# Reordering the first and last images of a fused GroupNorm, routed convolution and sign convolution kernel on one Trainium2 core

## What is computed

```python
# x = x + silu(bn(sum_e routing[b, e] * conv3x3(gn(x), w_experts[e])))
pooled = jnp.mean(x, axis=(2, 3))                       # x is gn(x) here
routing = jax.nn.sigmoid(pooled @ w_route.T + b_route)  # 4 experts
y = conv(x, w_experts)                                  # 3x3, 128 -> 4 * 128 channels
out = jnp.einsum('beohw,be->bohw', y, routing)
out = out * inv + (bn_beta - bn_mean * inv)
return jax.nn.silu(out)
# x = x + conv3x3(gn(x), sign(W))                       # 3x3, 128 -> 128 channels
```

## Time and profile before

| | us |
|---|---|
| median of 3 runs | 283.71 |
| lowest, highest of the 3 | 283.13, 285.51 |
| profiled execution, its own time | 283.86 |
| span of the profiled execution | 282.1 |
| TensorE busy (MATMUL records) | 270.5 (96%) |
| VectorE busy | 248.1 (88%) |
| ScalarE busy | 209.4 (74%) |
| GpSimd busy | 40.9 (15%) |

### The profile page before, as it was taken

One profiled execution on the slowest core, in us unless ns is written; L12 is line 12 of the kernel. 1 busy time (PEld: TensorE's weight loads), 2 busy tenths in 40 slices (PEclk: granted clock), 3 DMA queues, 4 the chain that ended last, 5 costly groups with the idle time before them and its releaser, 6 DMA issues.

```text
span 282.1 us, 3920 instructions
## 1 busy us (share of the span) xinstructions
PE 270.5 (96%) x1298; PEld 184.6 (65%) x1298; DVE 248.1 (88%) x443; ACT 209.4 (74%) x413; POOL 40.9 (15%) x58
## 2 busy tenths in 40 slices
PE   5599989999999999999999999999999999999896
PEld 5445755858576675858586776858586766757454
DVE  5697979899999999999999999999999999992832
ACT  2756888987879798988869898888878785618240
POOL 2100011212112021212123021212111031202000
PEclk9999999999999999999999999999999999999999
DMA  6999813461634544353625545353626455401312
GB/s 223 395 390 294 330 55 74 107 118 74 112 114 76 149 76 108 83 109 86 121 94 74 151 76 149 51 104 87 129 81 99 125 77 149 72 3 19 59 74 74
DMA packets 11252, 34.14 MB, mean 121 GB/s; under 512 B 1248, under 2 KB 3552, under 8 KB 11232
## 3 DMA queue, kind: packets, MB, share of 16 engines
q0 software_dynamic: 3888, 14.16, 29.6%
q1 hardware_dynamic: 7056, 19.47, 18.4%
q10 hardware_dynamic: 288, 0.26, 0.3%
HBM read 11.34 MB, written 15.73 MB: 96 GB/s over the span
## 4 chain that ended last, share of the span: by engine, by line
PE 78%; ACT 7%; issue 5%; DVE 5%; DMA 3%; POOL 1%; POOLq 0%; ACTq 0%; DVEq 0%
PE pc L457 35%; PE pa L422 12%; PE pe_ L422 11%; PE pb L422 11%; PE pd L412 6%; DMA X<-y 2%; DVE U L837 1%; ACT junk_mid L567 1%; DMA X<-x 1%; PE ps L395 1%; ACT hi L678 1%; DVE parts L803 1%; PE ps L390 1%; PE pb L457 1%; ACT dev L582 1%
## 5 line engine op out<-in xcount | busy, mean ns | idle before, releaser
L457 PE MATMUL pc<-lo,ws 128*128 128x496 f16 (+5 forms) x288 | 64.7, 371 | 0.0
L457 PE MATMUL pc<-hi,ws 128*128 128x496 f16 (+5 forms) x288 | 62.7, 372 | 1.0 <-ACT hi L678 1.0
L837 DVE SCALAR_TENSOR_TENSOR U<-we,route,U 128x1152 f32<-128x1152 f32 x45 | 63.4, 1410 | 0.1
L457 PEld LDWEIGHTS pc<-hi,ws 128*128 128x128 f16 x288 | 28.0, 98 | 32.3 <-issue 1.1
L457 PEld LDWEIGHTS pc<-lo,ws 128*128 128x128 f16 x288 | 28.3, 106 | 25.5 <-DVE lo L948 0.3
L422 PE MATMUL pa<-V,UM 128*128 128x256 f32 (+1 forms) x180 | 41.7, 382 | 0.0
L422 PE MATMUL pe_<-V,U 128*128 128x256 f32 (+1 forms) x180 | 40.6, 375 | 0.0
L422 PE MATMUL pb<-V,UM 128*128 128x256 f32 (+1 forms) x180 | 40.5, 375 | 0.0
L422 PEld LDWEIGHTS pb<-V,UM 128*128 128x128 f32 x180 | 34.2, 190 | 5.3 <-issue 0.4
L337 POOL TENSOR_TENSOR rstd<-ve,nhalf 128x2 f32<-128x2 f32 (+1 forms) x19 | 15.2, 803 | 154.0 <-ACT ve L595 154.0
L422 PEld LDWEIGHTS pe_<-V,U 128*128 128x128 f32 x180 | 34.1, 190 | 3.8
(11 more groups left out here) (97 smaller groups left out, 374.6 us busy)
## 6 DMA issues: line engine op xcount, KB each, us to landing
X<-x SPq DMA_DIRECT2D x15, 512.0 KB, 5.2
out<-X SPq DMA_DIRECT2D x14, 512.0 KB, 2.6
out<-ev POOLq DMA_DIRECT2D x14, 512.0 KB, 5.4
X<-y POOLq DMA_DIRECT2D x13, 512.0 KB, 4.6
we<-w_experts SPq DMA_DIRECT2D x3, 768.0 KB, 8.0
out<-X SPq DMA_DIRECT2D x3, 256.0 KB, 2.0
ws_raw<-w_sign SPq DMA_DIRECT2D x1, 576.0 KB, 11.5
X<-x ACTq DMA_DIRECT2D x2, 128.0 KB, 2.9
```

What stands on the lines that cost most here:

```text
L457: mm = mm_(rows[:, r0 - first // W:r1 - first // W, c0:c1], ws[:, tap * C:(tap + 1) * C], (hi, lo)[part][i % 2][:, r0 + ky - 1:r1 + ky - 1 ...
L837: v.scalar_tensor_tensor(out=flat(U[i % RING][:]), in0=flat(we[:, e, :, :]), scalar=route[:, i, e:e + 1], in1=flat(U[i % RING][:]), op0=AL ...
```

## The change

It touches the first 45 us of the program and its last image; the loop for t = 2 to 14 keeps its order on TensorE, ScalarE and GpSimd.

1. Dummy products: 9 at the start, 2 between `group_means(0)` and `group_vars(0)`, 4 behind `group_vars(0)`, 8 behind `route_logits(0)`. None stands behind `group_vars(1)` any more.
2. `group_means(1)` moves ahead of `route_logits(0)`. `group_vars(1)` moves behind the first two direct products (both halves of part 0).
3. VectorE forms `first_dev` and, from it and `rstd`, `pooled` of image 0 itself, instead of ScalarE's `zr` and `pool_routes(0)`. It also writes rows 17 to 31 of the first `xn` (`first_low_rows`), which ScalarE did. The five batch norm instructions are spread between the mixes of part 2. `pool_routes(2)` goes ahead of `mix(1, 3)`.
4. Image 0's second statistics on ScalarE: `squares`, `deviation` and the `IN` spread of chain 3 and `sign_weights` go ahead of `var_mid(0)`; `copy_minus(1)` comes last of them. `var_in(3)` moves from behind `mean_mid(0)` to ahead of `bias(2, IN)`. VectorE does `mix(2, 1)` before the inversion of image 1, no longer behind it, and `residual(0)` between `all_rows(2)` and `inner_rows(2)`. The first `hi` is written in two halves.
5. Image 14's residual moves from VectorE to the accumulating DMA (`DVE_RESIDUAL = (0, B - 1)`).
6. Last chain: ScalarE takes the sums from its Silu (`accum_out`), forms the mean (`last_mean`) and takes the variance in two halves (`last_variance`); VectorE's `part_stats` and `aggregate` of image 15 go away. On TensorE `group_means(18)` moves four products forward and `group_vars(18)` four.

```diff
-WARM = (7, 3)
+WARM = (9, 2, 4, 8)
...
-        DVE_RESIDUAL = (0, B - 2, B - 1)
+        DVE_RESIDUAL = (0, B - 1)
...
             group_means(0)
+            warm(WARM[1])
             group_vars(0)
+            warm(WARM[2])
+            group_means(1)
             route_logits(0)
-            group_means(1)
-            group_vars(1)
-            warm(WARM[1])
+            warm(WARM[3])
             direct_part(0, 0, 0)
             direct_part(0, 0, 1)
+            group_vars(1)
             direct_part(0, 1, 0)
...
+                elif t == B - 1:
+                    sign_half(t - 1, 0, 0)
+                    sign_half(t - 1, 0, 1, TAP_ORDER[:5])
+                    group_means(c + 1)
+                    sign_half(t - 1, 0, 1, TAP_ORDER[5:])
+                    sign_half(t - 1, 1, 0, TAP_ORDER[:5])
+                    group_vars(c + 1)
+                    sign_half(t - 1, 1, 0, TAP_ORDER[5:])
+                    sign_half(t - 1, 1, 1)
...
+            def last_mean():
+                i, c = B - 1, CHAINS - 1
+                act.wait_ge(silu_ready, silus(i) - 1)
+                activation(last_nm[:], ysum[:, i:i + 1], ACT.Identity, bias=nm[:, i, IN:IN + 1],
+                           scale=-1.0 / (HW * ROOT_HW)).then_inc(last_nm_ready, 1)
+                act.wait_ge(silu_ready, silus(i))
+                act.wait_ge(last_nm_ready, 1)
+                activation(nm[:, c, MID:MID + 1], last_ysum[:], ACT.Identity, bias=last_nm[:, 0:1],
+                           scale=-1.0 / (HW * ROOT_HW)).then_inc(nm_mid_ready, 1)
+
+            def last_variance():
+
+                i, c = B - 1, CHAINS - 1
+                act.wait_ge(nm_mid_ready, i + 1)
+                for half in range(2):
+                    act.wait_ge(h_ready, h_before(i) + half + 1)
+                    wait(act, var_mid_ready, i + half)
+                    activation(junk["mid"][:, 0:BANK], img(i)[:, half * BANK:(half + 1) * BANK], ACT.Square,
+                               bias=nm[:, c, MID:MID + 1], scale=1.0 / ROOT_HW,
+                               accum_out=(var[:, c, MID:MID + 1], last_var[:])[half]).then_inc(var_mid_ready, 1)
+                    if half == 0:
+                        squares(c)
+                        act.wait_ge(dev2_ready, columns_to(c))
+                        act.wait_ge(var_mid_ready, i + 1)
+                        activation(last_spread[:], dev2[:, c, MID:MID + 1], ACT.Identity, bias=var[:, c, MID:MID + 1],
+                                   scale=float(HW)).then_inc(last_spread_ready, 1)
+                act.wait_ge(last_spread_ready, 1)
+                act.wait_ge(var_mid_ready, i + 2)
+                activation(spread[:, c, MID:MID + 1], last_spread[:], ACT.Identity,
+                           bias=last_var[:, 0:1]).then_inc(spread_ready, 1)
...
             bias(0, IN)
-            pooled_plane(0)
             normalise_rows(0, 0, H // 2 + 1)
             routing(0)
             mix_first_part(0, 0)
+            mix_first_part(0, 1)
             deviations(1)
-            mix_first_part(0, 1)
-            normalise_rows(0, H // 2 + 1, H)
+            mix_first_part(0, 2)
             variance(1)
-            mix_first_part(0, 2)
             bias(1, IN)
             pooled_plane(1)
+            mix_first_part(0, 3)
             normalise(1)
-            mix_first_part(0, 3)
...
             variance(2)
+            var_in(3)
             bias(2, IN)
...
             mean_mid(0)
-            var_in(3)
+            squares(LAG)
+            deviation(LAG)
+            add_variance(LAG, IN)
+            sign_weights()
+            var_mid(0)
+            add_variance(LAG, MID)
+            copy_minus(1)
...
+            def first_routes():
+
+                dve.wait_ge(dev_ready, 1)
+                dve.wait_ge(route_prm_ready, 2)
+                v.tensor_scalar(first_dev[:], wroute[:], dev[:, 0:1], None, ALU.mult).then_inc(first_dev_ready, 1)
+
+            def first_pooled():
+                dve.wait_ge(first_dev_ready, 1)
+                dve.wait_ge(rstd_ready, 1)
+                v.scalar_tensor_tensor(out=pooled[:, 0, :], in0=first_dev[:], scalar=rstd[:, 0, IN:IN + 1],
+                                       in1=bshare[:], op0=ALU.mult, op1=ALU.add).then_inc(pooled_ready, 1)
+
+            def first_low_rows():
+                dve.wait_ge(nbias_in_ready, 1)
+                dve.wait_ge(zeroed, 3 + RING)
+                first = H // 2 + 1
+                v.tensor_scalar(xn[0][:, 1 + first:1 + H, :],
+                                img(0).rearrange("p (h w) -> p h w", h=H)[:, first:H, :], rstd[:, 0, IN:IN + 1],
+                                nbias[:, 0, IN:IN + 1], ALU.mult, ALU.add).then_inc(xn_low_ready, 1)
...
             part_stats(1, 0)
-            pool_routes(0)
+            first_routes()
             part_stats(1, 1)
-            aggregate(1, 1, IN, nm_in_ready, var_in_ready)
+            aggregate(1)
+            first_pooled()
+            first_low_rows()
...
             mix(1, 2)
+            pool_routes(2)
             mix(1, 3)
-            pool_routes(2)
...
-                transform_sums(t + 1)
+                all_rows(t + 1)
                 if t == 1:
                     residual(0)
+                inner_rows(t + 1)
                 transform(t + 1)
-                if t > 1:
-                    mix(t + 1, 1)
-                if t - 1 in DVE_RESIDUAL and t - 1 >= ND:
-                    residual(t - 1)
+                mix(t + 1, 1)
                 inverse_sums(t)
                 inverse_inner(t)
                 inverse_outer(t)
-                if t == 1:
-                    mix(t + 1, 1)
                 low_part(t - 1)
```

More of the change, by code:

```diff
@@ L405, in direct_part @@
                 last = part == len(DIRECT_PARTS) - 1
-                pe.wait_ge(xn_ready, 1 if i == part == half == 0 else i + 2)
+                pe.wait_ge(xn_ready, i + 1)
+                if i == 0 and half == 1:
+                    pe.wait_ge(xn_low_ready, 1)
                 pe.wait_ge(mixed, mixes_before(i) + (E - 1) * (part + 1))
@@ L668, in silu @@
                         part = flat3(y[i % 2][:, half * (TILES // 2):(half + 1) * (TILES // 2), :, :])
-                        activation(part, part, ACT.Silu, bias=bn_shift[:, 0:1], scale=bn_tiles[:, 0:1]) \
-                            .then_inc(silu_ready, 1)
+                        activation(part, part, ACT.Silu, bias=bn_shift[:, 0:1], scale=bn_tiles[:, 0:1],
+                                   accum_out=(ysum[:, i:i + 1], last_ysum[:])[half]).then_inc(silu_ready, 1)
             def split_hi(i):
@@ L676, in split_hi @@
                     act.wait_ge(conv_ready, 2 * (i - 1))
-                for first, last in ((0, H // 2 + 1), (H // 2 + 1, H)) if i == B - 1 else ((0, H),):
+                for first, last in ((0, H // 2 + 1), (H // 2 + 1, H)) if i in (0, B - 1) else ((0, H),):
                     activation(hi[i % 2][:, first:last, :], img(i).rearrange("p (h w) -> p h w", h=H)[:, first:last, :],
@@ L816, in pool_routes, with mix_part @@
                     v.scalar_tensor_tensor(out=pooled[:, c, :], in0=wroute[:], scalar=zr[:, c:c + 1], in1=bshare[:],
                                            op0=ALU.mult, op1=ALU.add).then_inc(pooled_ready, 1)
[L819 to L828 removed]
+            def mix_part(part, e):
+                n = (E - 1) * part + e - 1
+                if e == 1:
+                    dve.wait_ge(mix_first, part + 1)
+                else:
+                    dve.wait_ge(mixed, n)
+                u = kernel_part(U[0], part)
+                v.scalar_tensor_tensor(out=u, in0=kernel_part(we[:, e, :, :], part), scalar=route[:, 0, e:e + 1],
+                                       in1=u, op0=ALU.mult, op1=ALU.add).then_inc(mixed, 1)
@@ L937, in residual_last @@
                     v.tensor_tensor(part, rows, part, ALU.add).then_inc(h_ready, 1)
[L938 to L941 removed]
             def low_part(i):
                 dve.wait_ge(hn_ready, i + 1)
[L945 removed]
+                dve.wait_ge(hi_ready, his(i))
                 if i >= 2:
```

148 lines of the change are left out of this document (82 added, 66 removed).

## The result

| | before | after |
|---|---|---|
| median, us | 283.42 (4 runs) | 279.53 (4 runs) |
| lowest, highest, us | 283.06, 285.51 | 279.12, 283.74 |
| profiled execution, us | 283.86 | 279.12 |
| its span, us | 282.1 | 277.3 |

The ratio is 0.9838, interval 0.9805 to 0.9872; it leaves out the run at 283.74, which lies over 1.5% above the best of its kernel and has no trace. Two more groups timed the changed kernel again: medians 281.29 (6 runs, ratio 0.9895, 0.9857 to 0.9934) and 280.06 (6 runs, 0.9866, 0.9831 to 0.9901). All its 16 runs lie between 278.94 and 283.74 with a median of 280.3. That spread turned out to be half of the story.

What follows compares the result with a forecast made beforehand. TensorE was taken to bound the kernel, busy 188.94 of 189.00 us in the loop. From 283.86, 1.7 us (start), 0.6 and 0.85 (end) come off: 280.7 us, 1.06% under the median, range 279.2 to 283.8.

Steps and rivals of the forecast that it cites:

- F: Start of the first direct product on TensorE, 13.24 us before; forecast at 11.4 to 11.5.
- (f): Image 14's residual by DMA, at the end: TensorE's wait of 0.58 us for chain 17's spread goes.
- (g) and (h): Last chain's mean and variance: waits of 0.35 and 0.25 us remain, last image's products start 0.85 us earlier.
- (d): VectorE and ScalarE after the first direct product: most gain given back; minus points at 28.1 us, 2.4 earlier.
- (e): Image 0's second normalisation: TensorE waits 1.25 us for the spread; both engines enter the loop 1.7 us earlier.
- (c): First direct product: starts 1.8 us earlier; with full pace TensorE finishes the direct products some 3.3 us earlier.
- clock in between: Rival, chance 0.14: pace rises inside the eight dummies, product one at 13.0 to 13.5 us; total 282.7 us.
- (b): Image 0's route at the start: logits 0.3 us earlier or 0.35 later; mixing at 10.3 instead of 10.57.
- Late clock: Rival, chance 0.08: pace rises only at about 16.4 us, group_vars(1) stands behind slow direct passes; total 284.1 us.
- The end gives nothing beyond (f): Rival, chance 0.10: ScalarE's serial small steps at the end take 0.8 us more than forecast; total 281.5 us.
- The start gives 2.6 or more: Rival, chance 0.16: the start gains 2.6 us or more, as several forecast waits are sums of small steps; 279.7 us.
- The rule beside (a) and (c): TensorE's pace at the start: each run draws its own moment of rise; an early rise is likely, not sure.

Runs made afterwards that it cites:

- a_add14: Changed kernel with only image 14's residual back on VectorE: median 281.32 us.
- a_oldend: Changed kernel with the old end (image 14 added and image 15's statistics on VectorE, chain 18's sums in old places): median 281.66 us.
- a_stats15: Changed kernel with only the last chain's statistics back on VectorE and chain 18's sums in their old places: median 281.05 us.
- a_vars1first: Changed kernel with group_vars(1) back ahead of the first direct product, behind the eight dummies: median 279.63 us.
- a_wsearly: Changed kernel with sign_weights ahead of squares(3) on ScalarE: median 280.52 us.
- a_order0: Changed kernel with the old order around image 0's second normalisation on ScalarE and VectorE: median 278.97 us.
- a_late1: Changed kernel with the load of image 1 issued behind the first row of expert kernels (768 KB): median 283.93 us, ratio 0.9987.
- a_warm7003: Changed kernel with the old number of dummies (7 at the start, 3 ahead of the first direct product): 281.95 us, ratio 0.9931.
- a_route0: Changed kernel with image 0's pooled ahead of image 1's second statistics half, and its logits ahead of the eight dummies and group_means(1): 279.43 us, ratio 0.9855.
- b_dummies: Kernel before with dummy products alone added (9 at the start, 2 and 4 around group_vars(0), 3 kept): 284.03 us, ratio 1.0007.
- a_both: Changed kernel with image 0's route freed from image 1, ten starting dummies, and group_vars(1) between the halves of part 0: 278.63 us, ratio 0.9832.

## Why the prediction was right and wrong

**Right: what bounds, and the order of events.** The loop kept its length (204.4 us for thirteen turns), and nearly every step of the start fell near where it was put: first product 11.4 (measured 11.32), `ve` 13.5 (13.43), `e_rows` 17.3 (17.17), `pooled` 25.0 (24.63), minus points 28.1 (27.86), spread 34.85 (34.15), `hi` 37.8 (37.13), logits 42.4 (41.90). That VectorE and ScalarE give back part of the first product's gain was right: net of the 1.5 us that slow passes cost the old kernel, the path from F to image 2 grew from 33.6 to 34.77 us.

**Wrong: the sizes in the sum.** The mechanisms were right; the step that failed is the size of each term, since waits were priced at the idle time shown and small steps at their full length. Forecast were 1.7 for the start, nothing for the loop, 0.6 for (f) and 0.85 for (g) and (h), 3.15 us together. The two profiled executions differ by 2.20, 0.28, 0.84 and 1.42, together 4.74.

- *(f), 0.6 against 0.84* (252.97 to 256.49 became 250.49 to 253.17). The failing step is that the wait of 0.58 us "goes" at 0.58. Its idle time is counted from the modelled end of the last product, but without the wait the next one starts before that end: the minus points' row ends at 253.19, the sum starts at 253.03 and the plus points at 253.17. There the wait costs its idle time and 0.26 us, in a_add14 too (0.36 and 0.62).
- *(g) and (h), 0.85 against 1.42.* Here the sizes of the steps that remain failed. In the old times (3.32 us added, by the first `hi` products of image 14) TensorE did the sum of the mean at 264.77 where 264.95 was put (0.18), the sum of the spread 2.42 us later and not 2.5 (0.08), and the last `hi` 2.99 us after that and not 3.10 (0.11). This last is a slip in the sum: 267.45 and 2.8 us make 270.25 and not 270.55, and the 2.8 us in turn left out the sum's 0.24. The remaining 0.19 lies behind the last image's first product: TensorE no longer waits 0.17 us for `lo`, a wait that was not in the forecast. The waits of 0.35 and 0.25 us that it left at the two sums were 0.16 and 0.28 by the pace of the products.
- *The loop, nothing against 0.28.* 0.24 of it is chain 4's sum ahead of image 2's plus points: in the old order the minus points of image 2 and the plus points start 3.01 us apart, in the new one 2.77, and the rows show no idle time in either.
- *The start, 1.7 against 2.2.* In (d) the minus points came 2.65 us earlier and not 2.4, mainly since `pooled` of chain 2 came at 24.63. In (e) the spread's sum came 6.29 us behind the minus points and not 6.75, so the wait of 1.25 us was shown as 0.76: steps that were added up at full length took less.

**Wrong: one start.** Step (c) made F one number, and gave the "clock in between" 0.14. In four of the nine profiles of kernels with this start (both repeats, a_oldend, a_stats15) the dummies were slow, and in two more (a_add14, a_vars1first) image 1 landed late; early was F in the result's own, a_wsearly and a_order0. Step (b) counted as a gain that image 1's mean no longer waits for `pooled`; its other side, that `pooled` and the logits now wait for all of image 1's statistics and so for its load, was missed, and a_late1 shows that a later landing moves F by its full length. The two errors pull apart. The recorded 279.53 us comes from four runs of which three were at 279.12 to 279.93, early starts by their times, and lies 1.2 us below the forecast. The median of all 16 runs is 280.3; that 280.7 lies so near it is luck, since gains put too small and late starts left out cancel.

**The rivals.** *Late clock:* a_warm7003 shows its mechanism, direct passes at the slow pace with `group_vars(1)` behind them, but not its price, since there only three dummies stood ahead of F. The rival put 1.35 us behind F (31.5 less 13.5, against 28.1 less 11.45); a_warm7003 has 2.4 us there. With a late landing on top, a_late1 reaches the old time. *Clock in between:* its F of 13.0 to 13.5 came in both repeats, but they took 281.2 and 281.4 us and not 282.7: at image 2 they were 0.1 us ahead of and 0.1 us behind the kernel before, not 0.3 behind, and loop and end gave 2.5 us and not 1.45. *The end gives nothing beyond (f)* did not happen: the mean was there at 261.39, 2.27 us after the first Silu half's start where 2.51 was put. *The start gives 2.6 or more* was 2.2.

**The rule beside (a) and (c)** (the Trainium skill, TensorE: Matmul & The Clock Gate, Part 1: the number of slow products differs between runs of one kernel) held: the eight dummies ahead of the first product took 2.03, 3.74 and 3.76 us in three profiles of the same kernel. The forecast named it and then gave the slow starts too small a chance.

## What to carry to other kernels

Price a wait on a busy TensorE by the starts of its rows and not by the idle time that they show: set them beside a place where the same products and the same small sum run without waiting. Here each wait cost 0.16 to 0.26 us more than was shown, and some that cost up to 0.4 us showed nothing or little.

When work is put ahead of a critical step on an in-order engine, ask what that work itself waits for: a load that is usually early is a spread of several microseconds, not a constant. Dummy products helped here where TensorE did not run idle behind them and where they were through before the real product was ready. A gain of 1 to 2% whose start differs between runs has to be looked at as a distribution, of which four runs show little, or by stretches of the trace that repeat.

## What had not been expected of the hardware

GpSimd's power on 128x2 elements took 0.92 us on average over 13 in the kernel before and 1.72 in the changed one, with nothing changed in the instruction; single ones went from 0.70 to 2.0 us. The order of the streams alone does not decide it: the two repeats of the changed kernel have 1.82 and 1.52, a_stats15 and a_route0 with nearly the same order 0.73, and b_dummies with the old order 1.71. The loop hides it: 204.4 us with either. At the start it does not, as a_wsearly shows. What sets it was not tried.

A load of 512 KB issued at 2.1 us into the span landed 3.8 (a_route0) to 6.7 us (a_both) later in profiles of kernels that issue the same transfers in the same order.
